# Causal mask and row maxima of the first attention stage in one VectorE operation per head, with new call lists

## The reference, cut to what matters

```python
x = L0_attn_x                                   # (16, 256, 128)
xn = _layernorm(x, axis=-1)
x = x + _L0_attn_ref(xn, ...) + _L0_ffn_ref(xn, ...)

def _L0_attn_ref(x, Wq, bq, Wk, bk, Wv, bv, Wp, bp):
    q, k, v = (heads(Wq, bq), heads(Wk, bk), heads(Wv, bv))     # 16 heads of 8
    att = jnp.einsum('bhqd,bhkd->bhqk', q, k) * scale
    causal = jnp.tril(jnp.ones((t, t), dtype=bool))
    att = jnp.where(causal[None, None], att, -jnp.inf)
    att = jax.nn.softmax(att, axis=-1)
    y = jnp.einsum('bhqk,bhkd->bhqd', att, v)
    return y.transpose(0, 2, 1, 3).reshape(b, t, c) @ Wp.T + bp
```

## Time and profile before

| what | value |
|---|---|
| device time, median of three runs | 4661.67 us |
| span of the profiled execution, first to last instruction | 4655.4 us |
| sequences in this stage | 16 |
| last slot of maxima of the first sequence, turned at | 44.5 us |
| the same of the last sequence | 343.0 us |

### The profile page before, as it was taken

How to read it: one execution, slowest core, us unless ns; L and a number is a source line. 1 busy time by engine, 2 the same in 40 slices (tenths; PEclk the granted TensorE clock), 3 DMA queues, 4 the chain that set the end, 5 groups by cost and what they waited for, 6 DMA issues and landing times.

```text
span 4655.4 us, 137933 instructions
## 1 busy us (share of the span) xinstructions
PE 4360.4 (94%) x56640; PEld 2936.9 (63%) x56640; DVE 3703.2 (80%) x5128; ACT 3238.4 (70%) x6002; POOL 3648.6 (78%) x1951
## 2 busy tenths in 40 slices
PE   7889899978887999999999999999999999999998
PEld 4556688854443666666666666666666666666665
DVE  6874476759997888888888788888888788878885
ACT  4666655657774777777777777777777777777775
POOL 2223344469997999988999899989999898989993
PEclk9999999989998999999999999999999999999999
DMA  2000000023331222322233322323223222322222
GB/s 81 2 2 2 2 1 1 1 110 146 146 146 57 67 63 61 80 65 66 58 70 74 71 63 61 79 66 69 58 67 76 69 64 60 78 68 66 59 68 53
DMA packets 164376, 290.47 MB, mean 62 GB/s; under 512 B 44063, under 2 KB 61350, under 8 KB 159654
## 3 DMA queue, kind: packets, MB, share of 16 engines
q1 hardware_dynamic: 162310, 281.40, 23.2%
q10 hardware_dynamic: 1440, 0.24, 0.0%
HBM read 90.16 MB, written 2.62 MB: 20 GB/s over the span
## 4 chain that ended last, share of the span: by engine, by line
PE 57%; issue 4%; DVE 4%; DMA 2%; ACT 1%; SPq 1%; POOL 0%; DVEq 0%; ACTq 0%
PE ps L2626 19%; PE ps L2682 7%; PE ps L2639 7%; PE ps L2694 7%; PE ps L2655 5%; PE ps L2668 3%; PE ps L2720 3%; PE ps L2736 3%; PE ps L2727 3%; DMA L3f_vw<-L3f_v 2%; DVE L3f_ss L3019 1%; PE ps L2701 1%; PE ps L2707 1%; DVE L3f_raw L3036 1%; SPq L2472 1%
## 5 line engine op out<-in xcount | busy, mean ns | idle before, releaser
L3219 POOL TENSOR_TENSOR L3f_t<-L3f_raw,L3f_rot 128x1024 f32<-128x1024 f32 x384 | 1085.3, 2826 | 246.4 <-DVE L3f_raw L3036 242.8
L2626 PE MATMUL ps<-L3f_wqkv,all_z 128*128 128x512 f32 x2304 | 1154.1, 607 | 11.2 <-DVE L3f_raw L3036 8.8
L3236 POOL TENSOR_TENSOR L3f_raw<-L3f_raw,L3f_t 128x1024 f32<-128x1024 f32 x384 | 911.9, 2375 | 7.5
L3228 POOL TENSOR_TENSOR L3f_raw<-L3f_raw,L3f_rot 128x1024 f32<-128x1024 f32 x384 | 909.0, 2367 | 7.5
L2835 ACT ACTIVATE L3f_sqr<-ps 128x512 f32<-128x512 f32 x768 | 453.1, 595 | 295.8 <-PE ps L2626 292.4
L3036 DVE TENSOR_TENSOR L3f_raw<-ps,L3f_ri 128x512 f32<-128x512 f32 x768 | 498.7, 686 | 163.5 <-ACT L3f_ri L2845 154.4
L3019 DVE TENSOR_REDUCE L3f_ss<-L3f_sqr 128x8 f32<-128x512 f32 x768 | 515.6, 679 | 115.6 <-ACT L3f_sqr L2835 112.3
L2639 PEld LDWEIGHTS ps<-all_ident,L3f_raw 128*128 128x128 f32 x3072 | 363.3, 141 | 307.8 <-issue 270.3
L2626 PEld LDWEIGHTS ps<-L3f_wqkv,all_z 128*128 128x128 f32 x2304 | 395.8, 192 | 234.8 <-issue 180.2
L2639 PE MATMUL ps<-all_ident,L3f_raw 128*128 128x128 f32 x3072 | 474.5, 277 | 9.4 <-POOL L3f_raw L3236 3.7
L2682 PEld LDWEIGHTS ps<-L3f_pT,L3f_vw 128*64 128x64 f32 x12288 | 375.3, 138 | 97.0 <-issue 78.6
(11 more groups left out here) (332 smaller groups left out, 8632.4 us busy)
## 6 DMA issues: line engine op xcount, KB each, us to landing
L3f_vw<-L3f_v SPq DMA_DIRECT2D x1344, 128.0 KB, 2.4
L3a_Bs<-L3a_rows SPq DMA_DIRECT2D x16, 2048.0 KB, 7.1
L3a_Cs<-L3a_rows SPq DMA_DIRECT2D x16, 2048.0 KB, 11.7
L3f_vw<-L3f_v SPq DMA_DIRECT2D x192, 64.0 KB
L3f_wqkv<-in_L_ffn_Wqkv SPq DMA_DIRECT2D x24, 256.0 KB, 4.3
L3f_wqkv<-in_L_ffn_Wqkv SPq DMA_DIRECT2D x6, 512.0 KB, 4.2
L3f_wo<-in_L_ffn_Wo SPq DMA_DIRECT2D x48, 64.0 KB, 2.4
out<-all_x SPq DMA_DIRECT2D x8, 256.0 KB, 3.2
```

Source lines behind the costliest of these rows:

```text
L2626: p.matmul(PS[:, j % 3, :], Z[:, u % NSEQ, t * P:t * P + P], w, start=True, stop=True).then_inc(proj.sem)
L3219: g.tensor_tensor(t.rearrange("p h (b e) -> p h b e", b=2), r.rearrange("p h (b e) -> p h b e", b=2)[:, :, ::-1, :], w[:, 1, :].rearrange( ...
L3228: g.tensor_tensor(r, r, w[:, 0, :].unsqueeze(1).broadcast_to((P, H, HD)), ALU.mult).then_inc(cosined.sem)
L3236: g.tensor_tensor(r, r, t, ALU.add).then_inc(rotated.sem)
```

## The change

The mask products of the first scores are gone, and with them `cmaskb`. `cmask` is now 256 wide, zeros in front of the triangle, so that it serves both widths. `top` calls `tensor_tensor_reduce` once for each head: it adds the mask to the scores in PSUM, writes the sum back to PSUM, and puts the maximum into `mxe`. All four call lists are ordered anew, and TensorE's list begins one step earlier.

```diff
-        cmask = self.sb("cmask", [P, P])
-        cmaskb = self.sb("cmaskb", [P, P], BF16)
+        cmask = self.sb("cmask", [P, TILES, P])
...
+        nc.gpsimd.memset(cmask[:, 0, :], 0.0)
...
                     if 6 * (s + 1) + j:
                         p.wait_ge(s_max.sem, 6 * (s + 1) + j)
-                    for e in range(2):
-                        if j < 2:
-                            p.matmul(SP[:, e, :], self.identb[:, :], cmaskb[:, :].unsqueeze(1).broadcast_to((P, NM, P)), start=True, stop=False, skip_group_check=True)
-                        else:
-                            p.matmul(SP[:, e, :].rearrange("p (u k) -> p u k", u=2)[:, :, P:], self.identb[:, :], cmaskb[:, :].unsqueeze(1).broadcast_to((P, 2, P)),
-                                     start=True, stop=False, skip_group_check=True)
...
             both(k, 0)
+            values(k - 1, 1)
             values(k - 1, 2)
-            tx(k + 2)
+            both(k, 1)
+            qk(k + 2)
+            both(k, 2)
             fyp(k)
-            both(k, 1)
+            sl(k - 1)
+            both(k, 3)
             vp(k + 1)
-            sl(k - 1)
-            both(k, 2)
-            qk(k + 2)
-            both(k, 3)
-            values(k, 0)
             both(k, 4)
             project(k - 1)
             both(k, 5)
-            values(k, 1)
+            tx(k + 3)
             turn_max(k + 1)
+            values(k, 0)
...
-                if j < 2:
-                    op = v.tensor_reduce(to, SP.rearrange("p e (v k) -> p e v k", k=P), AX.X, ALU.max)
-                else:
-                    h = 1 - (j // 2 - 1)
-                    op = v.tensor_reduce(to[:, :, 2 * h:2 * h + 2], SP.rearrange("p e (v k) -> p e v k", k=SEQ), AX.X, ALU.max)
+                w, first = (P, 0) if j < 2 else (SEQ, 2 * (2 - j // 2))
+                hide = cmask[:, :, :].rearrange("p t k -> p (t k)")[:, SEQ - w:]
+                for e in range(2):
+                    for n in range(2 * SEQ // w):
+                        x = SP[:, e, n * w:(n + 1) * w]
+                        op = v.tensor_tensor_reduce(x, x, hide, 1.0, -3e38, ALU.add, ALU.max, to[:, e, first + n:first + n + 1])
...
-            top(k + 1, 1)
             quant(k + 1, 2)
+            top(k + 1, 2)
+            moments(k + 3, 1)
             kept(k, 1)
-            top(k + 1, 2)
+            top(k + 1, 3)
+            quant(k + 1, 3)
+            stats(k + 4, 0)
             value(k + 1)
-            stats(k + 4, 0)
-            quant(k + 1, 3)
-            top(k + 1, 3)
+            top(k + 1, 4)
+            quant(k + 2, 0)
             kept(k, 2)
+            top(k + 1, 5)
+            lower(k + 1, 0)
+            lower(k + 1, 1)
+            moments(k + 4, 0)
             stats(k + 4, 1)
             kept(k, 3)
-            top(k + 1, 4)
-            quant(k + 2, 0)
             residual(k - 1)
-            moments(k + 4, 0)
-            top(k + 1, 5)
-            quant(k + 2, 1)
-            lower(k + 1, 0)
-            lower(k + 1, 1)
             lower(k + 1, 2)
-            moments(k + 4, 1)
-            lower(k + 1, 3)
             top(k + 2, 0)
             kept(k + 1, 0)
+            quant(k + 2, 1)
+            lower(k + 1, 3)
+            top(k + 2, 1)
...
+        pe(-3)
         for k in range(-2, NSEQ + 1):
```

More of the change, by code:

```diff
@@ L221, in L0 @@
             NW += 1
-        for to, fr in ((hmask[:, :], d["c_head16"]), (spare[:, :], d["c_spare"]), (cmask[:, :], d["c_causal"]), (keep01[:, :], d["c_causal01"]),
+        for to, fr in ((hmask[:, :], d["c_head16"]), (spare[:, :], d["c_spare"]), (cmask[:, 1, :], d["c_causal"]), (keep01[:, :], d["c_causal01"]),
                        (bqk[:, 0:1], d["L0_attn_bq"].rearrange("(p a) -> p a", a=1)), (bqk[:, 1:2], d["L0_attn_bk"].rearrange("(p a) -> p a", a=1)),
@@ L248, in prepare @@
             v.tensor_copy(self.identb[:, :], ident[:, :])
-            v.tensor_copy(cmaskb[:, :], cmask[:, :])
             v.tensor_scalar(tmaskb[:, :], keep01[:, :], -1.0, -NEG, ALU.add, ALU.mult)
@@ L328, in score @@
                     if j < 2:
-                        mm = p.matmul(SP[:, e, n * P:(n + 1) * P], qm[r, b, NM - 1 - n, 0:P], km[r, b, NM - 1 - n, 0:P], start=False, stop=True, skip_group_check=True)
+                        mm = p.matmul(SP[:, e, n * P:(n + 1) * P], qm[r, b, NM - 1 - n, 0:P], km[r, b, NM - 1 - n, 0:P], start=True, stop=True)
                     else:
                         m = 2 * (j // 2 - 1) + 1 - n
-                        mm = p.matmul(SP[:, e, n * SEQ:(n + 1) * SEQ], qm[r, b, m, P:SEQ], km[r, b, m, :], start=False, stop=True, skip_group_check=True)
+                        mm = p.matmul(SP[:, e, n * SEQ:(n + 1) * SEQ], qm[r, b, m, P:SEQ], km[r, b, m, :], start=True, stop=True)
                 return mm
@@ L548, in act @@
             if k == NSEQ:
-                exponent(k - 1, 4)
                 exponent(k - 1, 5)
@@ L556, in act @@
                 return
-            exponent(k - 1, 4)
+            cast(k + 1)
             masked(k + 1, 1)
             exponent(k - 1, 5)
+            xt(k + 2)
             exponent(k, 0)
-            scaled(k)
-            xt(k + 2)
             out(k - 1)
             exponent(k, 1)
-            logarithm(k - 1)
             exponent(k, 2)
             ln(k + 3)
+            scaled(k)
+            root(k + 3)
+            logarithm(k - 1)
+            exponent(k, 3)
             inverse(k - 1)
-            root(k + 3)
-            exponent(k, 3)
-            cast(k + 2)
             masked(k + 2, 0)
+            exponent(k, 4)
         def dve(k):
@@ L729, in pool @@
             biased(k)
+            shared(k - 1)
             keep(k - 1)
@@ L732, in pool @@
             normed(k + 3, 1)
-            shared(k - 1)
             ffn(k)
```

## The result

The changed kernel takes 4711.64 us, the median of five runs (4687.59 to 4715.4), against 4662.54 us for the kernel before, also five (4660.33 to 4680.19). The ratio is 1.0095 with a 95% interval of 1.0069 to 1.012: 0.95% slower. The prediction was 4702 us. The profiled execution of the changed kernel took 4687.59 us, the shortest of the five, with a span of 4686.3 us, 30.9 above the span before.

The account below looks back on a forecast made before the run. The loop of VectorE's maxima and TensorE's scores through `SP` was taken as the bound. 10.95 + 11.36 = 22.31 us a sequence against 19.65 gave +40 us, 4702 us; eight times in ten between 4660 and 4775 us.

Parts of the forecast that it names:

- The loop through `SP`: VectorE's maxima and TensorE's scores wait for each other in turn through one buffer; 19.65 us a sequence before the change.
- The part outside the maxima: Per sequence, TensorE's part or VectorE's other work between maxima: 10.95 us after the change, against 12.27 before.
- Mask products: First-score mask products on TensorE's path: they delay scores by 0.52 us (slots 0, 1), 0.31 (2, 3), 0.22 (4, 5).
- The maxima: VectorE's masking and maxima in `top`, 32 instruction pairs a sequence: 6.88 + 32 f = 11.36 us, 3.98 more than before.
- f: What a pair (main instruction and write of the maximum) adds to its streaming in `top`: 0.14 us, edges 0.07 and 0.30.
- the point of balance: The f in `top` below which the change gains time: 0.057 us.
- The estimate from the Trainium skill: By the page's fixed costs a pair in `top` adds 0.185 us; maxima 12.8 us, run about 4724 us.
- The sum: 22.31 us a sequence against 19.65, +2.66 us, counted for 15 sequences: +40 us.
- The last step: From span to measured time: the median of the runs lies 6 us above the span of 4695, so 4702 us.
- The first sequence at no change: With TensorE at its lower level, mask products and maxima are dearer by as much: 0 us.
- The rival of the clock: TensorE, idling more, falls to 1.2 GHz; 6 us a sequence more, 4790 us or above; chance 0.06.
- One sign of being wrong: In the changed profile, added time in a clock below 1.00 between 60 and 340 us would show the prediction wrong.

## Why the prediction was right

The mechanism of the loop and of the pairs held. The agreement of the total is luck in part, and two smaller steps failed.

- *The loop through `SP`.* It bounds the stage before and after. Edits of `top` alone moved the steady length by 3.14 and 0.93 us. In the new lists the steps add up: +0.63 for the order, -1.62 for the mask products, +3.14 for the pairs, +2.15 in all.
- *The part outside the maxima.* Predicted 10.95 us, measured 21.86 - 2 x 2.10 - 4 x 1.64 = 11.10. Ahead of slots 5, 0, 1, 2, 3 and 4 it was 1.93, 2.91, 1.52, 1.45, 1.37 and 1.92, and no term was off by more than 0.13. In this sequence 0.81 us of constants for a later stage (214.93 to 215.74 us) stand ahead of slot 2; without them it is 1.37. Two readings behind these terms were inexact. The 0.57 us to `lower` came from a place where `lower` followed `quant` with no idle mark, so it was no measure of `turn_max`; the changed kernel, where `lower` does wait for it (206.45 to 206.98 us), has 0.53. And neighbours in the earlier trace rows overlap by 0.08 to 0.09 us (205.77 against 205.68), not 0.07.
- *Mask products.* 1.58 us predicted, 1.62 measured in the new lists. Their gain was real, and the pairs ate it. That the sums agree so well is luck: slots 2 to 5 gave 0.77 us in place of 1.06, and slot 0, counted at nothing, gave 0.31. In the old lists at full clock they are worth 19.65 - 18.99 = 0.66 us.
- *The maxima.* The term that was mis-sized is f: 0.14 us predicted, 0.116 measured. They took 10.76 us, not 11.36. The write of the maximum adds about 0.05 us beyond the 0.07 of the main instruction, less than two neighbours in the earlier trace rows. It hides in part, but not enough: the point of balance was 0.057. The estimate from the Trainium skill, page "VectorE: DVE Perf Modes", section on the TRN2 errata, was 0.185 us; the runs do not bear that out. The same page counts an accumulator output as two instructions (section on two Vector instructions with no wait between them), and the trace agrees: 512 and 512.
- *The sum.* +2.66 us a sequence predicted, +2.2 measured; 33 us in place of 40. The late start and the falls, put at zero in the sum, brought the stage back to 37.6. The last step, a median 6 us above the profiled span, didn't hold either: here the median lies 25 us above it. That the total of 4702 came within 10 us of 4711.64 owes something to these errors.
- *The first sequence at no change.* This step failed. Its premise (mask products and maxima both dearer at the lower level) missed that TensorE came to its higher level later. The first record of the full clock starts at 50.6 to 55.3 us in the five traces with plain reductions, and at 57.0 to 81.5 in the five with pairs. That the longer waits cause it is argued from this, not shown. In the first two sequences it cost 2.3 us in one profile and 7.1 in the other. With the falls, 4.9 and 8.5 us of the stage lie over the steady loss.
- *The rival of the clock.* Partly real: two falls of 3.4 us in the stage, near 95 and 361 us, not the lasting fall that 4790 us stood for. One sign of being wrong that the prediction named, a clock below 1.00 between 60 and 340 us, did come: the mean there is 0.99. The first comes behind a wait of 2.04 us; at 206.87 us the same `values` takes 1.07 us:

```profile
94.39 0.33 PE L382 MATMUL ps<-all_ident,L_mxe 128*128 128x128 f32 x1 [2.04 <-DVE L_mxe L622]
...
94.77 1.80 PE L399 MATMUL ps<-L_pT,L_vz 128*32 128x256 f32 x16
```

What the lists do was argued wrongly in part. The lists and the missing products together were credited with 1.32 us a sequence, and the lists alone lose 0.63 us. Beside the pairs they are even with the old ones in steady length; with plain reductions and no products they are 0.33 us shorter, mostly by the fill of slot 4. And the profiles with them have fewer falls: nine with the old lists, against two and one in the two profiles of the changed kernel, and eight against none where the maxima were plain reductions. Beside the pairs that is worth little: the stage takes 340.8 us with the old lists and 336.0 and 339.1 with the new ones, since the start differs too, and 2 to 5 us don't show in medians of runs that spread over 25 to 34 us (4707.13 and 4705.75).

What stays open is some 4 to 11 us. The medians differ by 45 to 49 us and the stage by 37.6 to 40.8. Behind the last turn the profiled executions took 4303 to 4332 us, whichever kernel it was, with mean clocks of 0.978 to 0.985; one execution of each kernel can't tell a part of the change in that from spread. The mean clocks of the changed kernel's runs (0.982 against 0.984) would account for some 8 us by the estimate above, but whether the change itself lowers the clock behind the stage isn't shown.

## What to carry to other kernels

Before masking is folded into a reduction that goes by head, count the instructions that one whole-slot reduction becomes: here each pair added 0.116 us to the same streaming, and 32 of them cost 3.1 us to save 1.6. Ask first whether the mask is needed at all; a maximum that only guards an exponential may be a bound that isn't too far above it. Leaving the mask out beat both versions in the new lists (0.9974), and made no difference in the old ones (0.9998). When a matmul is removed from a wait, look at the granted clock afterwards, since work in an idle stretch may be what keeps the other matmuls fast, as two traces here suggest.

## What the hardware showed that was not expected

- An accumulator's read, 0.14 us long in the trace, starts with the next main instruction, and a pair costs 0.116 us beyond its stream at both widths.
- TensorE's clock fell behind waits of 1.21 us ahead of slot 0 once the mask product no longer stood in them, and held behind a wait of 1.36 us in the changed kernel. In the kernel in which it fell, it also held behind the same wait of 1.21 us in other sequences (186.90 us). So the length of one wait doesn't tell it.
- The rise to 2.4 GHz in the first sequences came at about 53 us before, 64 in the first profile of the changed kernel and 82 in the second, of the same code (starts of the first record of the full clock; the matmul lengths above agree).
